# One core, attention beside a mixture of slots: the logits' matmuls stand before the scores, and VectorE empties them before the score maxima

## The reference

```
q, k, v = xn @ Wq, xn @ Wk, xn @ Wv        # 2 x 16 heads of 64
s = where(causal, q k' / 8, -1e30);  a = softmax(s)
o = a1 @ v1 - lam * (a2 @ v2);       attention = (0.2 * o) @ Wo
logits = (xn @ phi' + phi_b) as [row, 64 experts, 32 slots]
D = softmax over slots;  C = softmax over experts
X = D' @ xn -> clip, normalise, tanh;  Y = X @ expert_w + expert_b
slots = C @ Y
```

## Time and profile before

| | us |
|---|---|
| median of 3 runs | 1335.62 (1334.39 to 1339.07) |
| the profiled execution | 1331.79 |
| its span, first to last instruction | 1330.0 |
| TensorE busy | 1264.6 (95%) |
| VectorE busy | 1156.9 (87%) |
| GpSimd busy | 1098.1 (83%) |
| ScalarE busy | 1064.1 (80%) |

### The profile page before, as it was taken

One profiled execution on the slowest core, in us unless ns is written; L12 is line 12 of the kernel. 1 busy time (PEld: TensorE's weight loads), 2 busy tenths in 40 slices (PEclk: granted clock), 3 DMA queues, 4 the chain that ended last, 5 costly groups with the idle time before them and its releaser, 6 DMA issues. The chain is left out here.

```text
span 1330.0 us, 29570 instructions
## 1 busy us (share of the span) xinstructions
PE 1264.6 (95%) x9136; PEld 991.6 (75%) x9136; DVE 1156.9 (87%) x3632; ACT 1064.1 (80%) x3221; POOL 1098.1 (83%) x848
## 2 busy tenths in 40 slices
PE   2999999999999999999999999999999999489998
PEld 2777777777777777777777777777777777278887
DVE  7688999889988998899889988998899888877876
ACT  4788888898888888888888888888888888455554
POOL 1478888888888888888888888888888888859985
PEclk9999999999999999999999999999999999789999
DMA  6111122112211121122111221121111117357783
GB/s 174 50 57 71 70 75 72 71 70 82 72 70 70 59 72 70 71 75 78 67 69 70 82 72 70 71 82 64 64 62 67 69 70 214 96 198 247 248 266 119
DMA packets 105980, 126.31 MB, mean 95 GB/s; under 512 B 20192, under 2 KB 56032, under 8 KB 105696
## 3 DMA queue, kind: packets, MB, share of 16 engines
q1 hardware_dynamic: 102160, 122.97, 27.3%
q10 hardware_dynamic: 3664, 1.44, 0.5%
HBM read 48.89 MB, written 35.65 MB: 64 GB/s over the span
## 5 line engine op out<-in xcount | busy, mean ns | idle before, releaser
L722 ACT ACTIVATE e<-e,neg_max 128x256 f32<-128x256 f32 (+1 forms) x1024 | 451.5, 442 | 58.4 <-DVE neg_max L819 57.7
L819 DVE CUSTOM_DVE_ANT_0 e<-ps_s,mask 128x256 f32<-128x256 f32 (+1 forms) x1024 | 294.1, 351 | 66.9 <-PE ps_s L563 66.9
L1024 POOL TENSOR_TENSOR disp<-logit,gmax 128x512 f32<-128x512 f32 x128 | 134.4, 1050 | 190.8 <-DVE gmax L861 190.8
L1032 POOL TENSOR_TENSOR e<-e,inv 128x1024 f32<-128x1024 f32 x128 | 285.8, 2233 | 0.0
L563 PEld LDWEIGHTS ps_s<-qk 64*128 64x128 f32 x2048 | 172.9, 186 | 49.7 <-issue 45.2
L563 PE MATMUL ps_s<-qk 64*128 64x256 f32 (+1 forms) x2048 | 203.2, 337 | 0.0
L722 ACT ACTIVATION_READ_ACCUMULATOR e<-e,neg_max 128x1 f32 x1024 | 191.4, 187 | 0.0
L546 PEld LDWEIGHTS ps_t<-ident,e 128*128 128x128 f32 x1024 | 119.9, 141 | 68.6 <-issue 64.9
L1060 POOL TENSOR_TENSOR logit<-logit,m_all 128x512 f32<-128x512 f32 x128 | 165.0, 1289 | 0.0
L736 ACT ACTIVATE qk<-ps_t 128x512 f32<-128x512 f32 x126 | 75.3, 598 | 82.2 <-PE ps_t L80 77.1
L607 PE MATMUL ps_o<-pT,v_sb 128*64 128x256 f32 x1024 | 138.8, 392 | 0.0
(11 more groups left out here) (158 smaller groups left out, 3286.9 us busy)
## 6 DMA issues: line engine op xcount, KB each, us to landing
xs<-xT SPq DMA_DIRECT2D x128, 256.0 KB, 2.4
c_scratch<-logit SPq DMA_DIRECT2D x128, 256.0 KB, 2.0
xT<-c_scratch SPq DMA_DIRECT2D x16, 1024.0 KB, 5.5
c_back<-c_scratch SPq DMA_DIRECT2D x16, 1024.0 KB, 5.9
fx<-xT SPq DMA_DIRECT2D x64, 64.0 KB, 1.9
fxn<-xn SPq DMA_DIRECT2D x32, 64.0 KB, 1.9
xT<-in_L_ffn_expert_w SPq DMA_DIRECT2D x4, 512.0 KB, 6.7
xn<-in_L_ffn_expert_w SPq DMA_DIRECT2D x4, 512.0 KB, 7.1
```

What stands on the lines that cost most here:

```text
L722: ins = nc.scalar.activation(dst, dst, ACT.Exp, bias=neg_max[:, q, c:c + 1], scale=-1.0, accum_out=total[:, q, c:c + 1])
L819: nc.vector.tensor_tensor_reduce(out=dst, in0=part, in1=here, scale=-1.0, scalar=HIGHEST, op0=ALU.add, op1=ALU.min, accum_out=neg_max[:, q ...
L1024: nc.gpsimd.tensor_tensor(by_expert(bank_of(disp, t, jj)), by_expert(bank_of(logit, t, jj)), gmax[:, jj, :].unsqueeze(2).to_broadcast([P, ...
L1032: nc.gpsimd.tensor_tensor(e1[q][:], e1[q][:], inv[:, q, G:2 * G].unsqueeze(2) .to_broadcast([P, G, S]), ALU.mult).then_inc(norm_done, 1)
```

## The change

On TensorE the logits' three matmuls move from behind the products with v to a place ahead of the scores, and they use bank t1 in even steps and bank 0 in odd ones, where it was always bank 0. On VectorE `take_logits` moves from behind the maxima to a place ahead of them. The passes with a stride move too: `slot_max_end` and `slot_inverse` from j = 0 behind the maxima to j = 1 ahead of them, and `slot_sum`, still at j = 3, to a place ahead of them. Waits, other engines' orders and all sizes stay.

```
-        WO_BANK, LG_BANK = "t0", 0
+        WO_BANK, LG_BANK = "t0", ("t1", 0)
...
-                out = take_bank(LG_BANK, lg_out, 4 * t + j + 1)
+                out = take_bank(LG_BANK[j % 2], lg_out, 4 * t + j + 1)
...
+                if live(it, NTT):
+                    logits(it, j)
                 if live(v, NV):
                     scores(v, j, unit)
                 if v == NV + 1:
                     dispatch(LAST, 1)
                 if live(v - 2, NV):
                     output(v - 2, (j + 2) % 4, unit - 1)
-                if live(it, NTT):
-                    logits(it, j)
...
-                nc.vector.tensor_tensor(bank_of(logit, t, j), BANKS[LG_BANK],
+                nc.vector.tensor_tensor(bank_of(logit, t, j), BANKS[LG_BANK[j % 2]],
...
                     slot_max(*back(it, j, 1))
+                    if j == 1:
+                        slot_max_end(it - 1)
+                        slot_inverse(it - 3)
+                    elif it < ITER + 1:
+                        slot_sum(it - 2)
...
+                if live(it, NTT):
+                    take_logits(it, j)
                 if live(v, NV):
                     bank_max(v, j)
                 if live(g + 1, NG) and (kk, j) == (PER - 1, 2):
                     projections_low(nc, dve, env, g + 1)
-                if j == 0:
-                    slot_max_end(it - 1)
-                if j == 3:
-                    if it < ITER + 1:
-                        slot_sum(it - 2)
-                if j == 0:
-                    slot_inverse(it - 3)
-                if live(it, NTT):
-                    take_logits(it, j)
                 take_slots(it - 1, j)
```

## The result

The changed kernel takes 1397.46 us (median of 4 runs, 1396.0 to 1400.95), against 1335.01 for the one before in the same measurement: a ratio of 1.0471, with a 95% interval of 1.0448 to 1.0494. The change costs 4.7%. The forecast was 1402.

A forecast was written before the change was run, and what follows sets the result against it. TensorE, busy 95%, was taken to bound the kernel. New stalls of 83.6 us less the existing 16.7 gave + 67; with the tail, profiled execution 1400 and median 1402 us, range 1368 to 1434 (the forecast's own 1386 to 1414).

The forecast's parts named there:

- Part 1: Logits' place on TensorE: scores start 0.80 us later, step ends stay, and the 8.8 us of waits on emptied logits go.
- Part 2: Chain behind the maxima: odd steps' later exponentials delay the next Wo product, so each plain even step loses 0.30 us.
- Part 3: VectorE's emptying at j = 0 waits for GpSimd's addition ahead of the maxima: 1.5 us stall in each (it, 1).
- Group changes: Seven changes of weight group, put at 2.8 us each beyond the plain stalls, 19.6 us together; 2.2 each before.
- Tail: At (31, 2) the maxima queue behind take_logits, which waited 2.92 us for a store's DMA: + 1 to + 2 us.
- (a): Rival, chance 0.21: at j = 3 slot_max slips behind GpSimd's line 1032 and runs slowly, + 1.0 x 28, 1430 us.
- (b): Rival, chance 0.10: GpSimd's addition does not bind and only Part 2 holds, + 29, 1363 us.
- (c): Rival, chance 0.05: scores' chain has unseen slack, bank 0 waits and group-change stalls go; faster, about 1321 us.
- (d): Rival, chance 0.04: the order changes nothing since TensorE is full anyway, 1336 us.

The follow-up runs named there:

- The two experiments without the wait: Changed kernel with VectorE's emptying behind the maxima again at j = 0 only: 1362.4 us; changed kernel with GpSimd's additions one step earlier: 1369.05 us.
- the larger dose: Changed kernel with GpSimd's addition one operation later in each step, behind the dispatch weights (1.04 us): 1427.48 us, ratio 1.0698.
- the version that nearly reaches it: Kernel before, with the strided slot passes ahead of the maxima and the splits of new weights moved behind them: 1321.46 us, ratio 0.9902.
- the run with the early addition: Changed kernel with GpSimd's additions (add_banks) one step earlier, six steps back and not seven: 1369.05 us, ratio 1.0251.

## Why the prediction was right

The forecast and its order of causes held: 1397.5 where 1402 was put; for the profiled execution, 1400.95 where 1400 was put. By its steps:

- **Part 1.** The lengths 8.16 and 8.75 are the floor; plain steps of the changed kernel at j = 3 have the latter still, and the waits on the emptied logits are gone. Right.
- **Part 2.** Even steps lose 0.20, not 0.30. ScalarE's line 746 starts at T + 1.31 (559.36 - 558.05), I had 1.42; the Wo product starts at T + 2.87 (542.20 - 539.33), I had 2.97. The size was off by 0.1: I moved the scores by the logits' 0.80, but they start only 0.69 later when they follow logits instead of projections (odd steps without a stall have them at T + 4.83; before, T + 4.14), so that about 0.1 of the gap ahead of them is taken up. 0.1 on some 45 plain even steps is 4 us too much. That the mechanism is the odd step's scores is shown by the run with the new order in even steps alone, together with that of TensorE's order alone.
- **Part 3.** The addition ends at T + 7.14 (put at 7.17), the maxima start at T + 7.84 (7.8), the third projection at T + 4.18 of the next step (4.19). (The recorded terms add up to 12.62, not 12.65; that changes nothing.) The stall of a plain j = 1 step is 1.62, where 1.5 was put: the third projection is 1.5 late, and 0.1 more is lost right behind it, where the next matmul starts 0.34 after it instead of 0.23. The two experiments without the wait and the larger dose show it as cause.
- **Group changes.** Put at 2.8 each beyond plain stalls. The medians of the eight steps around one are 0.20, 1.62, 0.72, 0.88, 1.88, 0.86, 0.20, 0.01 from (4k-1, 0) to (4k, 3), and 0.81, 1.01 at (4k+1, 0) and (4k+1, 1): against plain steps 0.52 + 0.88 + 1.68 + 0.61 more, and 0.76 + 0.61 less, so 2.3. The j = 1 steps lose less there because the emptying finds the addition nearly done: at (4k, 0) it starts at T + 8.17 after 0.62 of waiting, where a plain j = 0 step has 2.47. Why (4k-1, 2), (4k-1, 3) and (4k, 0) lose what they do was argued from the splits, and no run takes it apart in the new order.
- **Tail.** Put at + 1 to + 2; it was + 6.1 in this execution, which is also the slowest of the four, 3.5 above their median. In the ten traces of this case it is 207.9 to 216.3, and the changed kernel's is within that. 2.1 of the 6.1 lie between line 688 and the first matmul of the last phase, in which TensorE was granted half its clock for a longer part. So errors of - 4 (even steps), + 3 (j = 1), - 3 (group changes) and + 4 nearly cancel; that the time came out closer than its terms is luck.
- **The rivals.** (a) did not happen where it was put: at j = 3 `slot_max` took 0.68 in every plain iteration and kept its place. (Its time for a `slot_max` that does lose it, T + 6.05, should be about 6.1.) But beside the group changes `slot_max` did miss the gap, which the forecast of 2.8 did not name: at (4k-1, 2), (4k, 0) and (4k+1, 0) it started 0.36 to 0.64 behind GpSimd's line 1030 and took about 2.1, 1.9 and 2.0 us, where before it started ahead of that operation and took at most 1.22. What this adds to the 2.3 was not isolated. (b) and (c) fall with the waits above, and (d) with the result.

## What to carry to other kernels

When an instruction is moved up in an engine's queue, all its waits move up with it, also those that never cost anything where it stood. List each of them with the time at which it is fulfilled in the trace before, and compare with the new place; here one of three, in one step of four, made more than half of the loss (without it, 35 of the 62 us came back). Where one engine bounds a phase, write down its step length without stalls first: it says what the best order can give (here 16 us), and here the version that nearly reaches it was found by taking away what delays the late engine and not by emptying banks sooner.

## What the runs showed of the hardware that was not expected

The clock fell behind short stalls of TensorE. In the run with the early addition TensorE waited 1.7 us ahead of the Wo product in each (4k, 0), and each (4k-1, 3) was 0.6 to 0.9 us too long. At three group changes of seven the granted clock then fell to the lower of its two levels, 1.2 instead of 2.4 GHz (the stretch from 179 to 182 us shows 0.53), and those steps took 11.8 us where the four others took 10.3. The waits of the seven are alike (1.68 to 1.70), so their length does not tell which of them cost the clock. The changed kernel waited 1.64 to 1.68 there, in steps 0.2 us shorter, and kept its full clock in the main phase at all seven; that the 0.2 us decide is not shown.

Between `slot_max` on VectorE and GpSimd's line 1030 the order of start decided. At (4k-1, 3) of that run `slot_max` started only 0.014 to 0.020 us ahead of line 1030 and still took 0.68, and line 1030 took 2.41. At (18, 0) of the same run it started 0.11 behind and took 2.33, and line 1030 took 1.89:

```profile
674.43 1.89 POOL L1030 TENSOR_TENSOR e<-e,inv 128x1024 f32<-128x1024 f32 x1
...
674.54 2.33 DVE L870 TENSOR_TENSOR m_run<-m_run,logit 128x512 f32<-128x512 f32 x1
```
